# First attention and feed-forward of a two-layer network: a new order of a turn, three PSUM banks for VectorE's products, waits block by block, stack rows six apart, the first keys split on VectorE

## The reference

```
x = LN(x + attention0(x))   # 16 heads of 8, rotary positions, causal softmax, out @ w_out.T
x = LN(x + ffn0(x))         # silu(x w1) * (x w2), gelu(. h1), gelu(. h2), w3; 512 hidden, ternary weights with scales
x = LN(x + attention1(x))   # 16 heads of 64, head mixing before and after a top-64 softmax, gates
x = LN(x + moe(x))          # 16 experts, top 4, and a shared one
```

## Time and profile before

| what | value |
|---|---|
| median of 3 runs | 3275.83 us (3272.88 to 3276.35) |
| profiled execution, its own time | 3288.68 us |
| its span | 3286.9 us |
| mean granted TensorE clock | 0.911 |
| PE busy | 2715.9 us, 83% |
| DVE, ACT, POOL busy | 2309.8, 2086.8, 1239.6 us |

### The profile page before, as it was taken

How to read it: one execution, slowest core, us unless ns; L and a number is a source line. 1 busy time by engine, 2 the same in 40 slices (tenths; PEclk the granted TensorE clock), 3 DMA queues, 4 the chain that set the end, 5 groups by cost and what they waited for, 6 DMA issues and landing times. The chain is left out here.

```text
span 3286.9 us, 59887 instructions
## 1 busy us (share of the span) xinstructions
PE 2715.9 (83%) x18884; PEld 1634.5 (50%) x18884; DVE 2309.8 (70%) x7740; ACT 2086.8 (63%) x5457; POOL 1239.6 (38%) x3658
## 2 busy tenths in 40 slices
PE   3678888888888888888888888888888888876898
PEld 1234333333333456555555555556556556555565
DVE  3445355444423399899799799899799888887465
ACT  0244655555453588788788788787787787874331
POOL 2111011101000256555565565565565565674000
PEclk6678889989889799999899999999999999987899
DMA  2111011001010211211211211211211211221342
GB/s 91 34 36 37 8 37 40 23 19 40 5 45 10 46 32 37 54 33 36 52 37 32 53 39 31 57 36 28 60 37 25 59 39 24 57 47 40 92 98 65
DMA packets 111295, 137.13 MB, mean 42 GB/s; under 512 B 20448, under 2 KB 90592, under 8 KB 110464
## 3 DMA queue, kind: packets, MB, share of 16 engines
q1 hardware_dynamic: 110976, 133.25, 17.8%
HBM read 47.62 MB, written 13.24 MB: 19 GB/s over the span
## 5 line engine op out<-in xcount | busy, mean ns | idle before, releaser
L1242 ACT ACTIVATE junk<-xs,thr 128x420 bf16<-128x420 f32 (+12 forms) x832 | 466.0, 570 | 74.8 <-POOL thr L957 59.8
L1083 PE MATMUL pt<-wsc,attn 128*128 128x128 f32 x2560 | 364.1, 292 | 101.9 <-POOL wsc L938 65.4
L1070 PE MATMUL pm<-mixin,pre_b 128*128 128x258 f32 (+15 forms) x1088 | 371.2, 457 | 91.2 <-ACT xs L1235 80.9
L1083 PEld LDWEIGHTS pt<-wsc,attn 128*128 128x128 f32 x2560 | 325.9, 200 | 192.7 <-POOL wsc L938 132.8
L615 DVE TENSOR_REDUCE row_max<-po 128x1 f32<-128x384 f32 (+3 forms) x352 | 209.5, 637 | 290.8 <-PE po L457 289.8
L1364 DVE MAX8 best<-left 128x8 f32<-128x420 f32 (+12 forms) x832 | 368.4, 483 | 0.0
L1036 PE MATMUL pa<-kT,qT 64*128 64x258 f32 (+3 forms) x1280 | 290.7, 457 | 85.6 <-ACT arena L1204 62.2
L1204 ACT ACTIVATE arena<-pa,nrm 128x258 f32<-128x258 f32 (+3 forms) x640 | 273.4, 477 | 105.1 <-PE pa L1036 99.4
L1394 DVE SCALAR_TENSOR_TENSOR attn<-xs,bound,ex 128x420 f32<-128x420 f32 (+14 forms) x480 | 226.6, 500 | 124.8 <-issue 62.0
L1070 PEld LDWEIGHTS pm<-mixin,pre_b 128*128 128x128 f32 x1088 | 179.9, 203 | 228.3 <-issue 198.0
L1261 ACT COPY at<-pt 128x128 f32<-128x128 f32 (+3 forms) x512 | 198.4, 450 | 114.7 <-PE po L1121 97.2
(11 more groups left out here) (235 smaller groups left out, 5960.8 us busy)
## 6 DMA issues: line engine op xcount, KB each, us to landing
spread<-gates_dram SPq DMA_DIRECT2D x32, 512.0 KB, 7.9
mixin<-arena SPq DMA_DIRECT2D x32, 258.0 KB
mixin<-arena SPq DMA_DIRECT2D x32, 242.0 KB
mixin<-arena SPq DMA_DIRECT2D x32, 226.0 KB
mixin<-arena SPq DMA_DIRECT2D x32, 210.0 KB
mixin<-arena SPq DMA_DIRECT2D x32, 194.0 KB
parts_dram<-parts SPq DMA_DIRECT2D x16, 384.0 KB, 3.9
q_stack<-parts_dram SPq DMA_DIRECT2D x96, 64.0 KB
```

Source lines behind the costliest of these rows:

```text
L1070: ins = nc.tensor.matmul(bank[:, 0:jn], pre_b[:, :], mixin[:, m % MIX_SLOTS, j0:j0 + jn], start=True, stop=not last)
L1083: ins = nc.tensor.matmul(bank[:, P * k:P * k + P], attn[:, m % A_SLOTS, P * k:P * k + P], wsc[:, m % A_SLOTS], start=True, stop=True)
L1242: ins = nc.scalar.activation(junk[:, z, 0:width(n)], xs[:, m % X_SLOTS, 0:width(n)], ACT.Sign, scale=-1.0, bias=thr[:, s % LIVE, z:z + 1], ...
```

## The change

1. `TURN` is written anew (both below). Per turn it has the same `C` and `V`; the `R` are dealt out 5, 3, 2, 1, 4, 3, 4, 0 instead of 5, 4, 2, 0, 4, 3, 4, 0; `f:1`, `f:2`, `f:3` follow one another and so do `h1:0` and `h1:1`; `start:1`, `den`, `x1T`, `mT:1`, `S` and `V` change places.
2. The o ring gets a third bank, which was one of the two for weighted values. The other now serves both halves, so that the first `V` of a half waits for the copy of the half before.
3. `hidden_1`, `hidden_2`, `down` and `project` wait for each block just before the matmul that reads it.
4. The eight rows of a slot lie six partitions apart (at slot, slot + 6, ...) and no longer beside each other.
5. For the first sequence DVE splits the keys, and ACT issues their thirteen transfers.

```diff
-        TURN = ("v R C R C V S1 R h2:2a R h2:2b C start:0 C R",
-                "C start:1 C R V den:1 h2:3 R C R C R y0",
-                "C x1 y1 C R V C x1T x2 R C",
-                "C mT:1 V f:0 C f:1 C f:2 C f:3 h1:0",
-                "C R C R V S0 h1:1a R h1:1b C R C",
-                "C R C V den:0 h1:2 C R C R",
-                "C R C R V h1:3a R h1:3b C R C",
-                "C mT:0 V C h2:0 C h2:1 C")
+TURN = ("R v R V C h2:2a h2:2b S1 R start:0 C R C start:1 C R",
+        "den:1 C R V C h2:3 C R C R y0",
+        "R C C x1 y1 V C R x2 C",
+        "R C V x1T C mT:1 f:0 C f:1 f:2 f:3 C h1:0 h1:1",
+        "R V C R S0 C R C R C",
+        "den:0 C R C h1:2 C R V C R",
+        "C R C h1:3a h1:3b R C R C R V",
+        "C mT:0 C V C h2:0 C h2:1")
...
-        banks_c, banks_o, banks_t = psum["a"] + psum["m"], psum["o"], psum["t"]
+        banks_c, banks_o, av_bank = psum["a"] + psum["m"], psum["o"] + psum["t"][:1], psum["t"][1]
...
+        def stack_rows(eng, b, z):
+            to, slots = ((q_stack, Q_PARTS), (k_stack, K_PARTS))[z]
+            for slot, part in enumerate(slots):
+                heads = parts_d[z][:, part * S:(part + 1) * S].rearrange("(a h d) s -> h d a s", h=2, d=HD0)
+                for hp in range(2):
+                    at = RB * hp + slot
+                    eng.dma_start(to[at:at + MAX_ROW:SLOTS, b % 2], heads[hp]).then_inc(stack_in, 16)
...
                 def values(b, n):
-                    if b and k == 0:
-                        pe.wait_ge(sums_done, 2 * (b - 1) + g + 1)
+                    if k == 0 and 2 * b + g:
+                        pe.wait_ge(sums_done, 2 * b + g)
...
                 def hidden_1(b, k, part):
-                    if k == 0 and part != "b":
-                        pe.wait_ge(o_free, O.nth(("f2", b, KC - 1)))
                     for j in range(KC // 2 if part == "b" else 0, KC // 2 if part == "a" else KC):
+                        if k == 0:
+                            pe.wait_ge(o_free, O.nth(("f2", b, j)))
...
+                act.wait_ge(keys_split, 1)
+                act.dma_start(parts_d[1], parts[:, 1].rearrange("p k s -> p (k s)")).then_inc(keys_out, 16)
+                act.wait_ge(keys_out, 16)
+                stack_rows(act, 0, 1)
...
+                def split_keys():
+                    dve.wait_ge(rot_done, 2)
+                    chain.link(nc.vector.tensor_copy(parts[:, 1, 0], rot[:, 1]))
+                    chain.link(nc.vector.tensor_tensor(rope_t[:, 0], rot[:, 1], parts[:, 1, 0], ALU.subtract))
+                    chain.link(nc.vector.tensor_copy(parts[:, 1, 1], rope_t[:, 0]))
+                    chain.link(nc.vector.tensor_tensor(rope_t[:, 0], rope_t[:, 0], parts[:, 1, 1], ALU.subtract))
+                    nc.vector.tensor_copy(parts[:, 1, 2], rope_t[:, 0]).then_inc(keys_split, 1)
```

More of the change, by code:

```diff
@@ L257, in plan @@
                 elif name == "h2":
-                    out += there("h2", b - (1 if n == CHUNKS - 1 else 2), int(arg[0]), arg[1:])
+                    out += there("h2", b - (1 if n >= TT else 2), int(arg[0]), arg[1:])
                 elif name == "h1":
@@ L316, in stack @@
                 def stack(b):
-                    for z, (to, slots) in enumerate(((q_stack, Q_PARTS), (k_stack, K_PARTS))):
-                        sp.wait_ge(parts_done, 2 * b + z + 1)
+                    for z in range(2) if b else range(1):
+                        sp.wait_ge(parts_done, split_nth(b, z))
                         if b:
@@ L321, in stack @@
                         sp.dma_start(parts_d[z], parts[:, z].rearrange("p k s -> p (k s)")).then_inc(parts_out, 16)
[L322 to L327, removed]
+                        sp.wait_ge(parts_out, 16 * split_nth(b, z))
+                        stack_rows(sp, b, z)
                 def row_parts(b, g):
@@ L378, in split @@
                     pool.wait_ge(rot_done, 2 * b + z + 1)
-                    if b:
-                        pool.wait_ge(parts_out, 16 * (2 * (b - 1) + z + 1))
+                    if b > 1 or b and not z:
+                        pool.wait_ge(parts_out, 16 * split_nth(b - 1, z))
+                    elif b:
+                        pool.wait_ge(keys_out, 16)
                     chain.link(nc.gpsimd.tensor_copy(parts[:, z, 0], rot[:, z]))
@@ L401, in _ @@
                 for what in PLAN:
-                    if what[0] == "start":
+                    if what[0] == "start" and what[1:] != (0, 1):
                         split(*what[1:])
@@ L475, in values @@
                             at = 2 * SUM_COLS * a
-                            ins = nc.tensor.matmul(banks_t[g][at:at + 2 * SUM_COLS, P * k:S],
+                            ins = nc.tensor.matmul(av_bank[at:at + 2 * SUM_COLS, P * k:S],
                                                    v_pad[:, b % 2, k, HS // 2 * g + a, SUM_COLS * odd:SUM_COLS * odd + 2 * SUM_COLS],
@@ L520, in hidden_2 @@
                 def hidden_2(b, k, part):
-                    if k == 0 and part != "b":
-                        pe.wait_ge(c_free, C.nth(("h1", b, KC - 1)))
                     bank = c_bank(("h2", b, k)) if part != "b" else banks_c[C.bank(("h2", b, k))]
                     for j in range(KC // 2 if part == "b" else 0, KC // 2 if part == "a" else KC):
+                        if k == 0:
+                            pe.wait_ge(c_free, C.nth(("h1", b, j)))
                         at = HID0 * j + P * k
@@ L601, in rotated @@
                 def rotated(b, z):
-                    if b:
-                        dve.wait_ge(parts_done, 2 * (b - 1) + z + 1)
+                    if b > 1 or b and not z:
+                        dve.wait_ge(parts_done, split_nth(b - 1, z))
+                    if b == 1:
+                        dve.wait_ge(keys_split, 1)
                     if 2 * b + z:
@@ L698, in _ @@
                         forms[what[0]](*what[1:])
+                    if what == ("start", 0, 1):
+                        split_keys()
         clear_semaphores(nc, sems)
```

19 lines of the change are left out of this document (12 added, 7 removed).

## The result

The changed kernel takes 3053.62 us (median of 4 runs, 3044.35 to 3063.46), beside 3276.09 us for the kernel before (3272.88 to 3276.89): a ratio of 0.9325, with an interval of 0.9299 to 0.9351. It is faster by 222 us. The forecast was 3149 us, 127 us faster, with a range down to 3110; the result lies outside the range, at the fast end.

What follows compares the result with a forecast made beforehand. PE sets the first phase's pace, losing time to standing and a clock at 0.90. Gains of 77 + 12 + 8 + 6 + 7 + 13 + 4 = 127 us from 3275.8 gave 3149 us, range 3110 to 3202.

Steps and rivals of the forecast that it cites:

- Turn 3: Round's second half, `f:0` to `h1:1`: `h1:0` waits for nothing, the 4.5 us wait and most likely 1.8 us slow clock go.
- Turns 4 to 7: Rest of the second half: 2.6 us of waits left; with turn 3, 59 us for 70, 11 us less, 77 over seven.
- First half: Round from `v` to `mT:1`: 2 us less each, 12 us over six, with a new 1.6 us wait after `y1`.
- Three banks: Ring of DVE's products: an `R` waits only for the first of two earlier reductions, 0.65 us earlier.
- The start: Keys' path before the first `R`: PE starts at 36.5 instead of 44.5 us, 8 us gained, bounds 2 to 11.
- The eleven `R`: First rows, 44.5 to 68.8 us before: three banks take 0.5 to 0.65 from each of ten cycles, 6 us.
- The 12.84 us wait: Sequence 0's `C` at 122.4 us, waiting for maxima sent behind the keys' transfers: 7 us gained, wait shrinking to about 6.
- (1): Rival, chance 0.2: the clock takes it; a second half gains 6 us, a first half nothing; 80 us gained, 3196 us.
- (2): Rival, chance 0.14: the clock follows the shorter waits upward; 14 and 4 us a half, 160 us gained, 3116 us.
- (3): Rival, chance 0.14: transfers no faster, ACT's share SP's rate; keys gain 2 us, sequence 0's wait nothing; 114 gained, 3162 us.
- (4): Rival, chance 0.03: slower than before, light stretches keep PE at 1.2 GHz through the hidden groups behind; 3311 us.
- (5): Rival, chance 0.03: no change, waits only move and a later transfer hides the start's gain; 3276 us.

Runs made afterwards that it cites:

- whole waits: Changed kernel with the four block-by-block waits undone, each layer waiting for the last block again: 3067.46 us, ratio 0.9359.
- the blocks apart: Changed kernel with a `C` between every two `f` of turn 3 again: 3083.55 us with waits by block, 3114.64 us with waits for the last block.
- one transfer: Changed kernel with each head's six slots laid out in DRAM and one transfer of 48 partitions replacing six of 8: 3049.63 us, ratio 0.9323.
- the two-bank kernel: Changed kernel with two banks instead of three in the ring of DVE's products, the third left unused: 3237.32 us, ratio 0.9856.

## Why the prediction was right, and where it was not

**What bounds the phase: right.** PE set the pace, and the round's 27.5 us come from the two things named, standing and the clock. The work of a round at full clock was put at 87 us and is 85.7. The clock's loss was put at 11.5 us; the busy time fell by 12.7.

**Turn 3: right.** The walk had `h1:0` wait for nothing, and 4.5 + 1.8 us go; the groups stand at 3.65 and 3.60 with no wait ahead. The order does nearly all of it: with whole waits the new order has a wait of 0.6 us there. With the blocks apart the waits by block take the wait from 4.56 to 1.77.

**Turns 4 to 7: right in the walk, wrong in what came after it.** The walk gave 52 us from `f:0` to the end of `h2:1`; 50.7 were measured. The step that failed is "I give the half three slow stretches, each slowing some hidden or value group by 1.7 us, so 5 us, and 2 us for what a walk leaves out: 59 us". The 7 us are not there: the clock is 1.00, PE runs none of the half at 1.2 GHz, and the half gained 19.3 instead of 11 us. I had taken the light stretches by themselves for the cause of the slow ones, and they stayed; what went was the waits in and ahead of them, as the 4.47 us right ahead of the slow group in the earlier trace rows. That waits matter is shown within the new order: filling them raised the clock, and a wait of 4.56 us put back brought a slow group back. Why a given wait is followed by a slow stretch is not shown: one of 1.77 us was with the old order and was not with the new.

**First half: the same error.** "2 us less each, 12" was a count of waits alone, with nothing for the clock; the half took 38.0 instead of 46.2 us, 8.2 less. The new wait of 1.6 us after `y1` is one of 0.98.

By stages the forecast comes to 8 us up to the first rows, 39 up to 322.4 (6 + 7 + 13, one second half of 11, one first half of 2), 65 in five rounds of 13, 11 in the last half and 4 at the end; measured were 8, 63, 135, 13 and 11. Of the 104 us too little, 70 lie in the five rounds: 14 us each. The forecast left 6 to 9 us of a round of 103 idle, so 94 to 97 busy; measured were 3.0 and 85.7. So the clock (with the work) is some 9 to 11 us of the 14 and the waits the rest. Another 24 lie ahead of them, where the clock is 0.99 from 128 us on instead of 0.84: the same cause.

**Three banks: a size right for the wrong place.** I counted 0.65 us for an `R`. It is there (6.9 with two banks in the new order, 2.4 with three), but about as much again is that `den`'s reciprocal (3.4 us, which I named only for the single bank of weighted values) no longer stands in the way of the `R` behind it: 6.0 us a round with two banks, none with three. Had I walked the new order with two banks, I would have met it.

**The start: right, in part by luck.** 36.5 us for the first `R` and 36.05 measured. The range of 33 (rate rises) to 41.5 (it does not) was the right question, and both parts were needed. But 36.5 was a value chosen between the two. The rate did rise; what kept the end from 33 is that ACT issues its twelve transfers until 33.8, a time I did not count. The eleven `R` behind took 18.9 us instead of 24.3, 5.5 less where I had 6. The 12.84 us wait: I had it shrink to 6; it moved, to the first `R` of sequence 1, and is 11.42. The longer issue alone does not explain that: with adjacent rows, issued in 4.1 us and moved more slowly, the wait is 10.68. From the rotated queries to this `R` it is some 30 us with either layout and 24 with one transfer, and PE, now faster, is through with its work before.

**The rivals.** (1), that the clock takes the gain, is refuted; the Trainium skill (TensorE: Matmul & The Clock Gate, "A second HAM failure mode: psum-queue depth-cycling"), on which I leaned for it, speaks of a PE that idles often for a short time between its groups of matmuls. The middle round of the changed kernel has seven waits, the longest of 1.0 us, 2.8 us in all, and a clock of 1.00; in the two-bank kernel, with the same items and 18.2 us of idle time, it is 0.88. So the trace agrees as far as idle time goes, and I had read the passage as if dense short items were idle time. (2), the clock upward, came nearest; its 14 and 4 a half were too small against 19 and 8, because I kept part of the slow stretches even there. (3) did not happen: six-apart rows move faster in two queues. (4) and (5) did not.

**What stays open.** Waits of 3.12 and 4.56 us were followed by a slow stretch; of those of 1.77 us one was and one was not; and one slow stretch began behind waits of 0.39 us. No rule is drawn from these places. Whether the old order lowers the clock by more than its waits was not tested: the old order with its waits filled would have told. What would lift the clock over the first rows was not found. And whether the 4 us between the changed kernel and the one with wide transfers are real could not be told.

## What to carry to other kernels

When a profile shows both waits and a mean clock below full, look for the slow stretch behind each wait and count it with the wait; and if an edit takes out nearly all the waits (here 17.8 to 3.0 us a round), give the clock at its full level a large chance in the forecast, rather than an average of before. Taking out a part of them need not help the clock: in the old order 15.0 to 10.1 us did not. Walk a new order against each resource it shares a part with: here the order was worth nothing with two banks and 136 us with three, and, for the first `R`, faster rows 0.3 us with one queue and 7.4 with two. A transfer laid out for bandwidth has to be priced at its issue as well.

## What the runs showed of the hardware that was not expected

- Work whose result nobody reads can pay: 10.7 us of matmuls a round, put into PE's waits, brought the last maxima 45 us forward (clock of a round 0.88, then 0.95 to 1.00).
- The clock can stand at 1.2 GHz behind short waits too: for 6 us behind one of 1.77 us, and in one round at 0.57 for 4 us behind two of 0.39, with PE busy in both stretches.
- The same 64 KB into eight partitions costs 0.34 us to issue when they are adjacent and 0.70 us when they stand six apart (12 in 4.1 and in 8.4 us), while the DMA engines' share falls from 0.58 to 0.43 and the rate rises from 85 to 134 GB/s. Into 48 adjacent partitions at once it was 168 GB/s at a share of 1.07.
- From 36 to 58 us, behind 4.59 us of idle time, 18.4 us of matmuls in 22 us did not lift the clock from 1.2 GHz; ahead of that idle time it had been full.
